# A transformer kernel with the filler matrix products at the heads of its attention stages removed

## The chip, the cores and the metric

The kernel runs on one core of one Trainium2 chip. The metric is device time in microseconds (us): the kernel before took 1113.98 us, the median of three runs (1110.98 to 1114.39). A core has five engines with queues of their own that meet only at semaphores: TensorE (PE in the profile, its weight loads PEld), VectorE (DVE), ScalarE (ACT), GpSimd (POOL) and SyncE (SP), which here only starts DMAs. TensorE's clock is granted at one of two levels, 1.2 or 2.4 GHz; the profile writes them 0.5 and 1.0.

## The reference

The input x is 2 x 1024 x 256 in float32; a context of 77 tokens per batch is attended to. Four layers follow each other, each with a cross attention and a feed-forward part:

```python
x = x + tanh(g_xattn[0]) * L0_xattn(layernorm(x), ctx)          # one head, no projections
x = x + tanh(g_ffn[0])   * L0_ffn(layernorm(x))                 # FP4 quantised gate, up, down
x = x + tanh(g_xattn[1]) * L1_xattn(layernorm(x), ctx, ctx)     # 16 heads of 16
x = x + tanh(g_ffn[1])   * L1_ffn(layernorm(x))                 # 256 -> 1024 -> 256, relu
x = x + tanh(g_xattn[2]) * L2_xattn(layernorm(x), ctx)          # 16 heads of 64
x = x + tanh(g_ffn[2])   * L2_ffn(layernorm(x))                 # one matrix, plus low rank
x = x + tanh(g_xattn[3]) * L3_xattn(layernorm(x), ctx, ctx)     # 16 heads of 16
x = x + tanh(g_ffn[3])   * L3_ffn(layernorm(x))                 # 16 experts and a shared one
```

An attention computes, per head, softmax(q k / sqrt(width)) v, and then an output projection.

## The kernel before

x stays in SBUF for the whole run, as 16 tiles of 128 rows. The program is a sequence of stages, and each engine runs through them in the same order: the start (layer 0's attention and the preparation of weights), `ffn0`, attention 1 (`att_tensor` and its fellows with l = 1), `ffn1`, attention 2 together with layer 2's feed-forward part (`att2_tensor` and its fellows), attention 3 (`att_tensor` with l = 3), and the mixture of experts. At the end of a stage each engine drains, raises a semaphore and waits until all five have done so (`end_stage`, L234 to L239; the profile shows these waits as L236).

Inside an attention stage each engine runs `pipeline` (L94): `step(t, p)` for t = -1, 0, 1, ... where `has(t)` tells whether a tile of that number exists. Steps up to 3 and the last ones are written out, the ones between run in a loop. The order of work on an engine is the program order, and there is no planner.

In `att_tensor`, step -1 turns the first normalised tile (two transposes, L373) and makes its queries (`queries`, L1216, eight products). ScalarE takes the queries' high part (`qT_hi`, L1304), VectorE the low part (`xT_lo`, L1351), and only then can the scores of tile 0 start. Step 0 turns tile 1, computes the scores of tile 0 in three pieces (`scores`, L1203, twelve products) and makes the queries of tile 1 (L1216). VectorE takes the maxima and subtracts them (L1362, L1363), ScalarE takes exponentials (L1319), and the low part of tile 1's queries stands in VectorE's order behind these. Step 1 begins with `wait_ge(tr_copied)` on exactly that low part. From step 1 on a step also turns the probabilities of the tile before (L373), multiplies them with the values (L1245), and from step 2 on projects (L1227, L1228).

In `att2_tensor`, step -1 turns the first tile (L1501); ScalarE makes `xT_hi` (L1545), VectorE `xT_lo` (L1608). Step 0 computes the scores of tile 0 (L1441, eighteen products) and turns tile 1 (L1501). Step 1 waits for tile 1's `xT_lo`. Later steps also turn the probabilities (L1451) and multiply them with the folded values (L1463).

At the end of a step with t < 1, and in `att2_tensor` also ahead of the pipeline, TensorE runs `keep_busy(pe, n)` (L884 to L887): n products of the bfloat16 tiles `ones3` (96 x 128) and two rows of `brow` (96 x 512) into bank 7 of PSUM. They wait for nothing, raise no semaphore, and nothing reads what they write: the next real product into bank 7 starts with `start=True`. There are 38 of them: 3 and 8 in attention 1 (steps -1 and 0), 4, 4 and 8 in attention 2 (ahead of the pipeline and in steps -1 and 0), 3 and 8 in attention 3.

Of the kernel before, what the change touches and what calls it, by code (L numbers as in the profile page):

```python
# [16 lines left out]
D = 256  # L17
# [65 lines left out]
def has(t):  # L83

    return not isinstance(t, int) or 0 <= t < T

def wait(eng, sem, value):

    if not (isinstance(value, int) and value <= 0):  # L90
        eng.wait_ge(sem, value)
# [21 lines left out]
def flamingo(nc, x_in, ctx_t, ctx_r, gates, tables, attn_in, bias_rows, fp4_in, ffn1_in, ffn2_in, moe_in,  # L113
             v_pairs, out):
    with ExitStack() as stack:
        enter = stack.enter_context

        def sb(name, shape, dt=F32):
            return enter(nc.sbuf_tensor(name, shape, dt))
# [7 lines left out]
        ones3 = sb("ones3", [96, P], BF16)  # L127
# [8 lines left out]
        brow = sb("brow", [96, NB * D], BF16)  # L136
# [83 lines left out]
        bank = [psum[:, 512 * n:512 * n + 512] for n in range(8)]  # L220
# [660 lines left out]

            return range((t - 1) * NPARTS // T, t * NPARTS // T) if 1 <= t <= T else range(0)

        def keep_busy(pe, n):  # L884

            for _ in range(n):
                pe.matmul(bank[7][:, 0:2 * D], ones3[:], brow[:, 0:2 * D], start=True, stop=True)  # L887

        def start_tensor(pe):
            s, tr, un = a_s[0], Count(), Count(set_s["filled"])  # L890

# [298 lines left out]
        def att_tensor(pe, l):  # L1190
            s, tr = a_s[l], Count()
            no, nt, vw = len(OUT_BANKS[l]), H * WIDTH[l] // P, VW[l]
            row = {1: 0, 3: 4}[l]

            def scores(t, p, j):
                h0, h1 = SCORE_BANKS[j]
                wait(pe, s["s_read"], 3 * t - 2 + j)
                col = (t // TB) * HK + h0 * SK
                parts = [(k, max(h0, 8 * k), min(h1, 8 * k + 8)) for k in range(KD)
                         if max(h0, 8 * k) < min(h1, 8 * k + 8)]  # L1200
                for k, a, z in parts:
                    for i, (q_, key) in enumerate(three((qT_hi[p], xT_lo[p]), (kb_hi[l], kb_lo[l]))):
                        last = pe.matmul(bank[j][:, (a - h0) * SK:(z - h0) * SK], q_[:, k, :],  # L1203
                                         key[:, bass.ds(col + (a - h0) * SK, (z - a) * SK)],
                                         start=(k, a, z) == parts[0] and i == 0,
                                         stop=(k, a, z) == parts[-1] and i == 2, skip_group_check=True)
                last.then_inc(s["s_ready"], 1)

            def queries(p, unit):

                pe.wait_ge(s["tr_copied"], unit)
                wait(pe, s["tr_copied"], tr.n - 1)
                dst = bank[TR34[tr.odd]]
                for j in range(KD):
                    for k in range(KD):
                        last = pe.matmul(dst[:, j * P:(j + 1) * P], Wq[l][:, k, j * P:(j + 1) * P], xnT[p][:, k, :],  # L1216
                                         start=j == 0 and k == 0, stop=j == KD - 1 and k == KD - 1,
                                         skip_group_check=True)
                last.then_inc(s["tr_filled"], 1)
                tr.up()  # L1220

            def project(t, unit):

                pe.wait_ge(s["tr_copied"], unit)
                wait(pe, s["y_read"], t - 2)
                for k in range(nt):
                    pe.matmul(bank[7][:, 0:D], onormT[:, k, :], Wo[l][:, k, :], start=k == 0, stop=False)  # L1227
                pe.matmul(bank[7][:, 0:D], ones3[:], brow[:, row * D:(row + 1) * D], start=False,  # L1228
                          stop=True).then_inc(s["y_ready"], 1)

            def values(t, p, units):

                v0 = ((t - 1) // TB) * KT * 3 * vw
                chunks = 0
                for g, k, a, z in value_items(l):
                    mine = [w[1] for w in value_items(l) if w[0] == g]
                    h0, a0 = OUT_BANKS[l][g][0], tile_heads(k)[0]
                    if k == mine[0]:

                        wait(pe, s["on_ready"], no * (t - 1) + g - 1)  # L1240
                    if k // 4 == chunks:
                        pe.wait_ge(s["tr_copied"], units[chunks])
                        chunks += 1
                    dst = bank[5 + (g + 1 - p) % 2][:, (a - h0) * vw:(z + 1 - h0) * vw]
                    last = pe.matmul(dst, probT[:, k, :],  # L1245
                                     Vb[l][:, bass.ds(v0 + (k * 3 + a - a0) * vw, (z - a + 1) * vw)],
                                     start=k == mine[0], stop=k == mine[-1], skip_group_check=True)
                    if k == mine[-1]:
                        last.then_inc(s["o_ready"], 1)

            def step(t, p):
                if has(t):
                    pe.wait_ge(s["tr_copied"], tr.n)
                if has(t + 1):
                    pe.wait_ge(s["xn_ready"], t + 2)
                    transposes(pe, s, tr, [(xn[1 - p][:, k * P:(k + 1) * P], P) for k in range(KD)], TR34)
                    xn_unit = tr.n
                if has(t):
                    scores(t, p, 0)
                    scores(t, p, 1)  # L1260
                if has(t - 2):
                    pe.wait_ge(s["on_ready"], t - 1)
                    transposes(pe, s, tr, [(onorm[:, k * P:(k + 1) * P], P) for k in range(nt)], TR34)
                    on_unit = tr.n
                units = []
                for j in range(3):
                    if has(t) and j == 1:
                        scores(t, p, 2)
                    if has(t - 1):
                        if j == 0 and isinstance(t, int) and t == 1:  # L1270
                            pe.wait_ge(pads_zero, {1: 4, 3: 6}[l])
                        if j == 0:
                            pe.wait_ge(s["exp_done"], t)
                        transposes(pe, s, tr, [(prob[1 - p][:, k * P:(k + 1) * P], P) for k in range(*PT_CHUNKS[j])],
                                   TR34)
                        units.append(tr.n)
                if has(t - 2):
                    project(t, on_unit)
                if isinstance(t, int) and t == T - 1:
                    front_turn(pe, l, 0)  # L1280
                if has(t + 1):
                    queries(1 - p, xn_unit)
                if has(t - 1):
                    values(t, p, units)
                if isinstance(t, int) and t == T - 1:
                    front_turn(pe, l, 1)
                if isinstance(t, int) and t == T:
                    for j in range(2, GT):
                        front_turn(pe, l, j)
                if isinstance(t, int) and t < 1:  # L1290
                    keep_busy(pe, 3 if t < 0 else 8)

            pipeline(pe, -1, step, [(tr, 2 * UNITS)], T + 1, AHEAD)
            if l == 3:
                router_logits(pe, 0)
            end_stage(pe, "pe")
# [134 lines left out]
        def att2_tensor(pe):  # L1431
# [52 lines left out]
            def step(t, p):  # L1484
                for j in range(3):
                    if has(t):
                        if j == 0:
                            pe.wait_ge(s["x_lo"], t + 1)
                        scores(t, p, j)
                    if j == 0 and has(t - 3):  # L1490
                        turn_second(t - 3)
                    if has(t - 1):
                        if j == 2 and isinstance(t, int) and t == 1:
                            pe.wait_ge(pads_zero, 6)
                        turn_probabilities(t - 1, 1 - p, j)
                if has(t - 3):
                    second(t - 3)
                if has(t + 1):
                    pe.wait_ge(s["xn_ready"], t + 2)
                    for k in range(KD):  # L1500
                        last = pe.transpose(x2_bank[:, k * P:(k + 1) * P], xn[1 - p][:, k * P:(k + 1) * P],  # L1501
                                            ident[:])
                    last.then_inc(s["x_filled"], 1)
                if has(t - 1):
                    outputs(t - 1, 1 - p)
                if isinstance(t, int) and t < 1:
                    keep_busy(pe, 4 if t < 0 else 8)

            keep_busy(pe, 4)
            pipeline(pe, -1, step, [(Count(), 0)], T + 2, AHEAD)  # L1510
            end_stage(pe, "pe")

# [1009 lines left out]
```

## Time and profile before

| | |
|---|---|
| median of three runs | 1113.98 us |
| profiled execution, its time | 1115.46 us |
| profiled execution, its span (first to last instruction) | 1113.7 us |
| mean granted clock of TensorE in it | 0.986 |
| TensorE busy | 1049.1 us (94%), 6222 products |
| VectorE busy | 786.0 us (71%) |
| ScalarE busy | 517.6 us (46%) |
| heads of the attention stages, first filler product | 270.7, 500.5, 677.1 us |

The page cuts the span into 40 slices of 27.8 us and gives each engine's busy share in tenths. The timeline and the windows used below have times in us from the start of the span. A busy time of TensorE counts overlapping products once. In the timeline, products of one form that stand next to each other are merged, so a row has a start, the length of the whole, and the count; "[0.71 <-DVE xT_lo L1351]" at the end says that the engine was idle for 0.71 us before it and what released it.

### The profile page before, as it was taken

Reading aid. Unit: us, or ns where it says so; the run is one execution under the profiler, and the core shown is the slowest. Engines: PE = TensorE matmul, PEld = TensorE weight load, DVE = VectorE, ACT = ScalarE, POOL = GpSimd, SP = SyncE. Lnnn points to the kernel's source line nnn. Section 1 sums busy time; section 2 is a strip of 40 time slices with the busy share of each in tenths; the row PEclk is TensorE's granted clock in tenths of the full one; section 3 lists DMA queues with packets and bytes.
Section 4 is the critical chain, followed back from the end, with each engine's and each line's share of the span. In section 5 each row is a group of like instructions: output and inputs, shape, how many; then the busy total and the mean of one; then the engine's idle time right before and its main releaser. Section 6 shows DMA issues by size and latency. Waiting matters only on the chain.

```text
span 1113.7 us, 18644 instructions
## 1 busy us (share of the span) xinstructions
PE 1049.1 (94%) x6222; PEld 899.6 (81%) x6222; DVE 786.0 (71%) x1809; ACT 517.6 (46%) x1196; POOL 164.1 (15%) x227
## 2 busy tenths in 40 slices
PE   4887899998999999999999997999989999999998
PEld 3755567776999978887888886999868888888887
DVE  5787879987787845458888867888655575565544
ACT  3676544433555555545544543565542433333322
POOL 2232000000112142230111001123331010000000
PEclk9899899999999989999999999999999999999999
DMA  9401010002000000000000005000022121222120
GB/s 277 113 1 41 1 12 1 1 1 77 1 1 0 2 12 1 1 1 1 1 0 0 1 1 241 1 0 1 1 73 66 54 78 56 58 75 64 51 86 29
DMA packets 30376, 41.22 MB, mean 37 GB/s; under 512 B 13615, under 2 KB 19577, under 8 KB 29414
## 3 DMA queue, kind: packets, MB, share of 16 engines
q1 hardware_dynamic: 29437, 39.63, 11.4%
q10 hardware_dynamic: 873, 0.72, 0.3%
q8 instruction: 39, 0.64, 0.2%
q14 instruction: 27, 0.22, 0.1%
HBM read 37.80 MB, written 2.54 MB: 36 GB/s over the span
## 4 chain that ended last, share of the span: by engine, by line
PE 51%; DVE 2%; ACT 1%; DMA 0%; issue 0%; PEldq 0%; POOL 0%; DVEq 0%; POOLq 0%; SPq 0%; PEld 0%; ACTq 0%
PE psum L2082 17%; PE psum L2093 8%; PE psum L1463 6%; PE psum L1441 5%; PE psum L1245 3%; PE psum L1203 3%; PE psum L373 2%; PE psum L1451 2%; PE psum L1227 1%; PE psum L1216 1%; PE psum L1480 1%; PE psum L2037 0%; PE psum L1501 0%; DMA work<-expert_shares 0%; PE psum L1472 0%
## 5 line engine op out<-in xcount | busy, mean ns | idle before, releaser
L298 POOL TENSOR_TENSOR rstd<-ve,mhalf 128x1 f32<-128x1 f32 x128 | 83.5, 653 | 697.2 <-DVE ve L293 697.2
L384 ACT COPY work<-psum 128x256 f32<-128x256 f32 (+2 forms) x241 | 99.5, 438 | 134.9 <-PE psum L373 130.0
L373 PE MATMUL psum<-ident,work 128*128 128x128 f32 (+2 forms) x596 | 97.2, 287 | 14.6 <-DVE xT_lo L1351 4.3
L2225 DVE TENSOR_TENSOR work<-psum,work 128x512 f32<-128x512 f32 x68 | 46.9, 690 | 74.8 <-ACT work L2156 74.7
L2164 ACT CAST h_hi<-work 128x512 fp32r<-128x512 f32 x68 | 42.2, 621 | 122.1 <-DVE work L2235 95.4
L373 PEld LDWEIGHTS psum<-ident,work 128*128 128x128 f32 (+2 forms) x596 | 74.5, 149 | 28.8 <-DVE xT_lo L1351 6.2
L2082 PE MATMUL psum<-x_hi,ew_hi 128*128 128x512 f32 (+1 forms) x272 | 87.2, 402 | 0.2
L2082 PE MATMUL psum<-x_lo,ew_hi 128*128 128x512 f32 (+1 forms) x272 | 85.3, 395 | 0.0
L2082 PE MATMUL psum<-x_hi,ew_lo 128*128 128x512 f32 (+1 forms) x272 | 84.9, 393 | 0.0
L1662 PE MATMUL psum<-early,work 128*128 128x352 f32 x256 | 81.4, 473 | 3.3 <-ACT zone L597 2.8
L2093 PE MATMUL psum<-ew_hi,h_hi 128*128 128x256 f32 x272 | 76.4, 281 | 2.3 <-DVE h_lo L2242 2.3
L2093 PE MATMUL psum<-ew_hi,h_lo 128*128 128x256 f32 x272 | 76.7, 282 | 0.0
L2093 PE MATMUL psum<-ew_lo,h_hi 128*128 128x256 f32 x272 | 76.3, 281 | 0.0
L2242 DVE TENSOR_TENSOR h_lo<-work,h_hi 128x512 fp32r<-128x512 f32 x68 | 47.0, 690 | 41.6 <-ACT h_hi L2164 41.5
L1245 PEld LDWEIGHTS psum<-zone,work 128*128 128x128 f32 x640 | 74.0, 192 | 0.2
L1245 PE MATMUL psum<-zone,work 128*128 (+2 forms) x640 | 74.2, 273 | 0.0
L1662 PEld LDWEIGHTS psum<-early,work 128*128 128x128 f32 x256 | 49.0, 197 | 29.2 <-ACT zone L597 3.6
L2156 ACT ACTIVATE work<-psum 128x512 f32<-128x512 f32 x68 | 40.6, 597 | 68.8 <-PE psum L2082 68.5
L1463 PE MATMUL psum<-zone,work 128*128 128x256 f32 (+1 forms) x320 | 71.7, 379 | 0.0
L1463 PEld LDWEIGHTS psum<-zone,work 128*128 128x128 f32 x320 | 59.6, 190 | 7.6
L1531 ACT ACTIVATE work<-psum,small 128x77 f32<-128x77 f32 x256 | 62.5, 380 | 3.9 <-DVE small L1565 3.9
L1362 DVE TENSOR_REDUCE small<-psum 128x6 f32<-128x462 f32 (+1 forms) x96 | 55.6, 580 | 9.0 <-PE psum L1203 9.0
(275 smaller groups left out, 2543.2 us busy)
## 6 DMA issues: line engine op xcount, KB each, us to landing
work<-expert_shares SPq DMA_DIRECT2D x64, 256.0 KB, 3.2
early<-in_experts_in SPq DMA_DIRECT2D x1, 6528.0 KB, 18.0
x<-in_x_in SPq DMA_DIRECT2D x4, 512.0 KB, 7.8
early<-in_W_in SPq DMA_DIRECT2D x2, 1024.0 KB, 6.0
out_x<-x SPq DMA_DIRECT2D x3, 512.0 KB, 4.3
early<-in_Wk SPq DMA_DIRECT2D x1, 1024.0 KB, 7.2
early<-in_Wq SPq DMA_DIRECT2D x1, 1024.0 KB, 9.0
zone<-in_Wv SPq DMA_DIRECT2D x1, 1024.0 KB, 13.8
```

What stands on the lines that cost most here:

```text
L298: pool.tensor_tensor(rstd[:, slot:slot + 1], ve[:, slot:slot + 1], mhalf[:, 0:1], ALU.pow).then_inc(s["rstd_ready"], 1)
L373: last = pe.transpose(dst[0:rows, at:at + n], src, ident[0:n, 0:n])
L384: act.copy(dst, src).then_inc(s["tr_copied"], 1)
L1245: last = pe.matmul(dst, probT[:, k, :], Vb[l][:, bass.ds(v0 + (k * 3 + a - a0) * vw, (z - a + 1) * vw)], start=k == mine[0], stop=k == min ...
L1362: link(dve, dve.tensor_reduce(mx[:, h0:h1], sc, AX_X, ALU.max))
L1441: last = pe.matmul(bank[j][:, 0:n], x_[:, k, :], a[k][0][:, bass.ds(col + a[k][1], n)], start=i == 0 and k == 0, stop=i == 2 and k == KD - 1)
L1463: pe.matmul(bank[6][:, 0:D], probT2[p][:, k, :], vo[:, bass.ds(v0 + k * D, D)], start=k == 0, stop=False, skip_group_check=True)
L1531: last = act.activation(prob[p][:, h * SK:(h + 1) * SK], bank[j][:, (h - h0) * SK:(h - h0 + 1) * SK], ACT.Exp, bias=nmx[:, h:h + 1])
L1662: last = pe.matmul(bank[c][:, 0:HALF], xnT[1 - p][:, k, :], wguT[:, k, c * HALF:(c + 1) * HALF], start=k == 0, stop=k == 1)
L2082: last = pe.matmul(bank[2 * which + e % 2][:], weights(w, e, which, k), a[:, k, cols], start=n == 0, stop=n == len(passes) - 1)
L2093: last = pe.matmul(bank[6 + j // 2][:, (j % 2) * D:(j % 2 + 1) * D], h[slot(e)][:, j * P:(j + 1) * P], weights(w, e, 2), start=e == 0 and ...
L2242: dve.tensor_tensor(h_lo[slot(e)][:], hf[e % 2], h_hi[slot(e)][:].bitcast(F32), ALU.subtract).then_inc(s["h_ready"], 1)
```

## The change

The calls of `keep_busy` in both functions and its definition are taken out. Nothing else changes.

```diff
-        def keep_busy(pe, n):
-
-            for _ in range(n):
-                pe.matmul(bank[7][:, 0:2 * D], ones3[:], brow[:, 0:2 * D], start=True, stop=True)
@@ step of att_tensor, at its end
-                if isinstance(t, int) and t < 1:
-                    keep_busy(pe, 3 if t < 0 else 8)
@@ step of att2_tensor, at its end, and ahead of its pipeline
-                if isinstance(t, int) and t < 1:
-                    keep_busy(pe, 4 if t < 0 else 8)
-
-            keep_busy(pe, 4)
             pipeline(pe, -1, step, [(Count(), 0)], T + 2, AHEAD)
```

## Rows read from the trace of the kernel before

**Rows 1.** The page: busy time of each engine, and the slices of TensorE's clock.
```profile
PE 1049.1 (94%) x6222; PEld 899.6 (81%) x6222; DVE 786.0 (71%) x1809; ACT 517.6 (46%) x1196; POOL 164.1 (15%) x227
PEclk9899899999999989999999999999999999999999
```
**Rows 2.** Windows: stretch, length, busy us per engine, TensorE's clock (PEclk), DMA share, GB/s.
```profile
285.00:380.00 95.00, 95.00 (x753) 90.90 (x753) 76.71 (x190) 49.75 (x102) 14.49 (x22) 1.00 0.00 1
```
**Rows 3.** Instructions of L887: duration in ns, minimum, median, maximum.
```profile
L887 PE MATMUL psum<-brow,ones x38: 376/379/390, 270.7 to 683.1; 96*128 96x512 bf16 x38
```
**Rows 4.** Timeline at the head of attention 1, TensorE.
```profile
268.79 0.44 PE L373 MATMUL psum<-ident,work 128*128 128x128 f32 x2 [0.63 <-DVEq L236]
...
269.75 1.16 PE L1216 MATMUL psum<-work,zone 128*128 128x128 f32 x8 [0.52 <-ACT work L384]
...
272.26 0.44 PE L373 MATMUL psum<-ident,work 128*128 128x128 f32 x2 [0.71 <-DVE xT_lo L1351]
...
274.36 1.05 PE L1216 MATMUL psum<-work,zone 128*128 128x128 f32 x8
...
278.55 0.44 PE L373 MATMUL psum<-ident,work 128*128 128x128 f32 x2 [1.41 <-DVE xT_lo L1351]
```
**Rows 5.** Timeline at the head of attention 2, TensorE and one row of VectorE.
```profile
500.52 1.04 PE L887 MATMUL psum<-brow,ones 96*128 96x512 bf16 x4 [2.06 <-SPq L236]
...
500.88 0.41 DVE L313 TENSOR_SCALAR work<-x,rstd,small 128x256 f32<-128x256 f32 x1
...
501.39 0.38 PE L1501 MATMUL psum<-ident,work 128*128 128x128 f32 x2
...
502.75 0.70 PE L1441 MATMUL psum<-a_hi,xT_hi 128*128 128x462 f32 x2
...
506.23 0.38 PE L1501 MATMUL psum<-ident,work 128*128 128x128 f32 x2
506.45 1.89 PE L887 MATMUL psum<-brow,ones 96*128 96x512 bf16 x8
...
509.59 0.68 PE L1441 MATMUL psum<-a_hi,xT_hi 128*128 128x462 f32 x2 [1.25 <-DVE xT_lo L1608]
```
**Rows 6.** Timeline at the head of attention 3, TensorE.
```profile
680.67 1.05 PE L1216 MATMUL psum<-work,zone 128*128 128x128 f32 x8
...
684.88 0.44 PE L373 MATMUL psum<-ident,work 128*128 128x128 f32 x2 [1.43 <-DVE xT_lo L1351]
```
**Rows 7.** Windows of stretches in which TensorE waited; columns as in rows 2.
```profile
82.90:86.30 3.40, 0.90 (x6) 0.56 (x4) 3.23 (x9) 0.86 (x5) 2.55 (x7) 1.00 0.00 0
...
127.30:130.70 3.40, 1.39 (x7) 0.77 (x5) 3.30 (x6) 3.24 (x10) 0.00 (x0) 1.00 0.00 0
803.20:806.60 3.40, 1.75 (x8) 1.08 (x9) 1.37 (x4) 2.41 (x5) 0.00 (x0) 1.00 0.00 0
86.40:89.80 3.40, 3.40 (x12) 3.09 (x13) 2.37 (x6) 2.58 (x9) 0.00 (x0) 0.50 0.00 0
820.30:823.70 3.40, 1.68 (x8) 1.02 (x6) 1.49 (x5) 0.77 (x2) 0.04 (x1) 1.00 0.79 278
499.40:502.80 3.40, 2.17 (x11) 1.00 (x11) 2.74 (x9) 0.37 (x1) 0.76 (x3) 1.00 0.03 7
```
**Rows 8.** Timeline of TensorE at the head of ffn1: the clock rises at 403.8.
```profile
401.02 1.06 PE L1881 MATMUL psum<-xg_lo,w_hi 128*128 128x512 f32 x2
401.88 1.06 PE L1881 MATMUL psum<-xg_hi,w_lo 128*128 128x512 f32 x2
...
404.64 0.63 PE L1881 MATMUL psum<-xg_hi,w_hi 128*128 128x512 f32 x2
405.10 0.63 PE L1881 MATMUL psum<-xg_lo,w_hi 128*128 128x512 f32 x2
```
**Rows 9.** Windows, columns as in rows 2: the longest stretch at the low clock after the start.
```profile
45.50:52.20 6.70, 6.70 (x30) 6.59 (x30) 1.43 (x6) 2.58 (x7) 0.28 (x1) 0.50 0.00 0
```
**Rows 10.** The window's products against the identity (transposes): length, TensorE, its weight loads, clock, DMA.
```profile
55.70:59.10 3.40, 2.12 (x15) 1.37 (x14) 1.00 0.00 0
```

## The prediction

> **What bounds the kernel now.** I read the page first: TensorE is busy for 94% of the span, and its clock is at the full level in nearly every slice [rows 1]. The windows over the running part of attention 1 say the same: TensorE is busy for 95.00 of 95 us, VectorE for 76.71 [rows 2]; attentions 2 and 3 look alike. So once a stage is under way, whatever TensorE loses there arrives at the end. The heads of the stages are different. There the timeline shows TensorE waiting for VectorE, and the removed products stand in these waits, so I looked at three things: how long each wait would be without them, what the granted clock did elsewhere after such waits, and what a stretch at the low clock costs.
>
> **The removed work by itself.** 38 products of 379 ns [rows 3]; next to each other they start about 0.22 us apart (eight in 1.89 us, 1.89 - 0.38 = 1.51 over seven steps [rows 3, 5]). That is 38 x 0.22 = 8.4 us of array time. None of it is on the path, with one exception:
> - Attention 1, step -1: after the three fillers TensorE still waits 0.71 us for `xT_lo`; step 0: after the eight it still waits 1.41 us [rows 4].
> - Attention 3, step 0: still 1.43 us [rows 6], and its step -1 repeats attention 1's.
> - Attention 2: 1.25 us is left after the eight [rows 5], and the four of step -1 end some 0.3 us before the scores start at 502.75.
> - The exception is the four ahead of the pipeline: they start at 500.52 and the transposes behind them at 501.39, 0.87 us later. But the tile that these turn is written from 500.88 to 501.29 [rows 5], so the transposes can start only 0.1 us earlier.
>
> Cost of the work itself: a gain of 0.1 us, between 0 and 0.87. Nothing waits on the fillers, no semaphore or DMA moves, and the wait that ends each stretch stays the same `xT_lo`. If this were all, nothing measurable would happen.
>
> **What takes the fillers' place: idle time.** Ends and starts from rows 4 to 6:
> - Attention 1, step 0: the queries end at 274.36 + 1.05 = 275.41, the next product starts at 278.55: 3.14 us.
> - Attention 3, step 0: 681.72 to 684.88: 3.16 us.
> - Attention 2, step 0: 506.61 to 509.59: 2.98 us.
> - Attention 2, head: TensorE has been idle since 500.52 - 2.06 = 498.46; from there to 502.75, in 4.29 us, only two transposes of 0.38 us are left.
> - Step -1 of attentions 1 and 3: from 268.79 - 0.63 = 268.16 to 272.26, 4.1 us with 0.44 + 1.16 = 1.60 us of work, in attention 3 the same.
>
> **What the clock does after such waits.** At the full level, stretches of 3.4 us in which TensorE was busy for 0.90, 1.39 and 1.75 us were each followed by a fall to 1.2 GHz, one of 1.68 us was not, and the head of attention 2, with its fillers at 2.17 us, was not [rows 7]. None of the waits of before at the full clock is as long as the three bare ones above: with them, a stretch of that length holds under 0.5 us of work if it lies on the wait, less than in any of rows 7. So I expect a fall at each step 0 and at the head of attention 2, and about an even chance in each step -1, whose 1.60 us lies between the row that fell at 1.75 and the one that held at 1.68.
>
> The Trainium skill ("TensorE: Matmul & The Clock Gate", section on why this matters) advises against idle gaps of more than about 3 us; two of the bare waits are just over, one is just under. Read strictly it would leave these falls in doubt; that is the first rival. The trace is harsher than the page: the wait in 82.90 to 86.30 was 2.5 us, and the clock fell. The same page (part 4) says that transposes don't count as the engine's work in the way products do. Read so, step -1 would hold only the queries' 1.16 us and fall more surely. The trace doesn't bear that out: in 55.70 to 59.10 TensorE's work was 2.12 us of transposes and hardly anything else, and the clock stayed at 1.00 [rows 10]. I leave the chance even.
>
> **What a fall costs.** The shortest stretch at the low clock is 3.4 us, as 86.40 to 89.80, where TensorE is then busy throughout [rows 7]. The same pair of 512-column products starts every 0.86 us at the low clock (401.02, 401.88) and every 0.46 us at the full one (404.64, 405.10) [rows 8]. A fully used stretch of 3.4 us thus does 3.4 x 0.46 / 0.86 = 1.8 us of full-clock work: it loses 1.6 us. If part of it lies in the wait, that part costs nothing; if the engine finds too little to do, the low clock goes on for 6.7 us [rows 9] and costs up to 3.1 us.
> - Each step 0: the fall comes inside the wait or shortly after its end; then step 1 keeps TensorE busy without a stop. Between 0 and 3.1 us; I take 1.2, three quarters of the 1.6, as about a quarter of the stretch should lie in the wait. Three times: 3.6 us.
> - Head of attention 2: the scores of tile 0, 502.75 to 506.23 at the full clock, run at half. Behind them stand the maxima, the exponentials and `xT_lo` of tile 1, which ends the next wait, so nearly the whole delay goes on. Between 0 and 3.1 us; I take 1.3.
> - Step -1 of attentions 1 and 3: the scores of tile 0 slow down, but VectorE's chain behind them is as long as they are. 0.6 us each when it falls, half the time: 0.6 together (0 to 3.1).
> - The fillers themselves: -0.1.
>
> Sum: 3.6 + 1.3 + 0.6 - 0.1 = 5.4 us. Against the profiled execution's own time of 1115.46 that is 1120.9. The median of the timed runs lies 1.5 us lower, so I forecast **1119.4 us**. By the lower bounds the sum is -0.9, by the upper ones 3 x 3.1 + 3.1 + 3.1 = 15.5.
>
> **Rivals.**
> - *The clock holds* (for it: 820.30 to 823.70 held with 1.68 us of work [rows 7]; against it: the bare waits hold far less). Then only -0.1 is left: 1113.9 us.
> - *Falls, but mostly hidden*: they come early in the waits, or at steps where VectorE is the slower one anyway (71% busy overall [rows 1]). Two falls of 1.2 us remain: 1116.3 us.
> - *The low clock stays on*: the heads have more waits, so a fallen clock finds too little work to rise again, as in 45.50 to 52.20 [rows 9]. Four places at 3.1 us: 12.4 us, 1126.4 us. Step 1 with its unbroken work speaks against it.
> - *Faster*: by earlier or later starts the falls that before has at stage ends (as after 803.20 to 806.60 [rows 7]) vanish, at 1.6 us each; there are four such in the trace, at the ends of attentions 1 and 3 and the stages behind them. This decides only if all bare waits also stay without a fall and at least three of these go: 1109.1 us. Those falls stem from waits that the change doesn't touch.
> - *Nothing happens because the fillers did nothing*: the same as the first rival, and counted there.
>
> **How the numbers follow.** A difference under 0.3% (3.3 us, so 1110.6 to 1117.3) can't be told from none. Chances: forecast 0.64 (own range 1117.3 to 1124), clock holds 0.13, mostly hidden 0.12, stays low 0.07, faster 0.04. Slower: 0.64 + 0.07 = 0.71; within: 0.25; faster: 0.04. The range 1113.0 to 1124.0 takes in the forecast, the hidden case and most of the first rival; outside are the low clock that stays, the faster case, and the edges.
>
> **What would show it.** Right: the windows over 277 to 284, 500 to 514 and 683 to 690 of the new trace have PEclk 0.50 for 3.4 us or more each; the timeline has idle times of about 3.1, 3.0 and 3.2 us before the first product of step 1; the first step of each stage is 1 to 2 us longer, and the later steps are unchanged. Wrong: the idle times are there and the clock stays at 1.00 in two or more of the four places, or it falls and the step's end is not later, which would make VectorE the path at the heads.

## The result and the profile after

| | before | after |
|---|---|---|
| median | 1113.75 us (6 runs, 1110.83 to 1114.39) | 1119.20 us (6 runs, 1118.36 to 1120.28) |
| profiled execution | 1115.46 us | 1119.74 us |
| span | 1113.7 us | 1117.9 us |
| mean granted clock | 0.986 | 0.979 |

The ratio after to before is 1.0061, with a 95% interval of 1.0047 to 1.0075. The medians differ by 5.4 us. The ratio, by which noise is judged, stands for 6.8 us (5.2 to 8.4): slower, clear of noise, by well under 2%.

The page after, its first part and the clock; they answer to [rows 1]. TensorE has 38 products less, and two more slices, the 10th and the 25th, have a lower clock digit.

```profile
PE 1048.3 (94%) x6184; PEld 901.6 (81%) x6184; DVE 785.7 (70%) x1809; ACT 517.4 (46%) x1196; POOL 164.1 (15%) x227
PEclk9899899998999989999999998999999999999999
```

Timeline of TensorE at the heads of the three stages after (start, length, what, count, idle time before it and what ended it). The rows answer to [rows 4], [rows 5] and [rows 6]; ten lines were taken out, so `scores` of attention 1 is L1198 now, `queries` L1211, and attention 2's transposes and scores are L1494 and L1434.

```profile
268.79 0.44 PE L373 MATMUL psum<-ident,work 128*128 128x128 f32 x2 [0.63 <-DVEq L236]
269.74 1.16 PE L1211 MATMUL psum<-work,zone 128*128 128x128 f32 x8 [0.52 <-ACT work L384]
272.26 0.69 PE L373 MATMUL psum<-ident,work 128*128 128x128 f32 x2 [1.36 <-DVE xT_lo L1344]
...
276.08 1.91 PE L1211 MATMUL psum<-work,zone 128*128 128x128 f32 x8
279.51 0.45 PE L373 MATMUL psum<-ident,work 128*128 128x128 f32 x2 [1.51 <-DVE xT_lo L1344]
...
286.68 0.41 PE L373 MATMUL psum<-ident,work 128*128 128x128 f32 x2
...
501.34 0.44 PE L1494 MATMUL psum<-ident,work 128*128 128x128 f32 x2 [2.06 <-SPq L236]
503.36 1.12 PE L1434 MATMUL psum<-a_hi,xT_hi 128*128 128x462 f32 x2 [1.58 <-DVE xT_lo L1598]
...
508.39 0.38 PE L1494 MATMUL psum<-ident,work 128*128 128x128 f32 x2
511.44 0.68 PE L1434 MATMUL psum<-a_hi,xT_hi 128*128 128x462 f32 x2 [2.67 <-DVE xT_lo L1598]
...
676.96 0.44 PE L373 MATMUL psum<-ident,work 128*128 128x128 f32 x2 [0.69 <-POOLq L236]
...
680.44 0.44 PE L373 MATMUL psum<-ident,work 128*128 128x128 f32 x2 [1.36 <-DVE xT_lo L1344]
...
687.32 0.44 PE L373 MATMUL psum<-ident,work 128*128 128x128 f32 x2 [2.17 <-DVE xT_lo L1344]
...
695.92 0.42 PE L373 MATMUL psum<-ident,work 128*128 128x128 f32 x2
```

The queries of tile 1 took 1.05 us [rows 4] and take 1.91 now, and the first pair of attention 2's scores took 0.70 [rows 5] and takes 1.12. That is the low clock. The windows of the same profile show its stretches (stretch, length, busy time of the engines, then TensorE's clock):

```profile
271.30:278.10 6.80, 5.73 (x22) 5.28 (x22) 4.37 (x10) 0.71 (x4) 0.00 (x0) 0.50 0.59 248
503.40:506.80 3.40, 3.40 (x9) 2.97 (x10) 0.74 (x2) 0.07 (x1) 0.20 (x1) 0.50 0.00 0
680.90:684.30 3.40, 3.40 (x14) 3.26 (x14) 2.19 (x4) 0.37 (x1) 0.00 (x0) 0.50 0.74 323
687.70:691.10 3.40, 3.40 (x15) 3.19 (x14) 2.06 (x4) 0.37 (x1) 0.00 (x0) 0.50 1.12 481
```

Where the time of this execution went can be read stage by stage, from a stage's first product to the first product of a later step:

| from, to | before | after | longer by |
|---|---|---|---|
| attention 1: first transposes to step 1 | 268.79 to 278.55 | 268.79 to 279.51 | 0.96 |
| the same to step 2 | to 285.56 | to 286.68 | 1.12 |
| attention 2: first product to step 1 | 500.52 to 509.59 | 501.34 to 511.44 | 1.03 |
| attention 3: first transposes to step 1 | 675.12 to 684.88 | 676.96 to 687.32 | 0.60 |
| the same to step 2 | to 691.89 | to 695.92 | 2.19 |

1.12 + 1.03 + 2.19 = 4.3 us, and the spans differ by 4.2 us. The rest of the kernel gave and took a few tenths. The rows of the timeline of before that the table and the experiments need, and that are not among [rows 4] to [rows 6] (first products of step 2 of attention 1, of attention 3, and of step 2 of attention 3; 514.16 is the turn of tile 2 in step 1 of attention 2):

```profile
285.56 0.42 PE L373 MATMUL psum<-ident,work 128*128 128x128 f32 x2
...
514.16 0.38 PE L1501 MATMUL psum<-ident,work 128*128 128x128 f32 x2
...
675.12 0.44 PE L373 MATMUL psum<-ident,work 128*128 128x128 f32 x2 [0.69 <-POOLq L236]
...
691.89 0.42 PE L373 MATMUL psum<-ident,work 128*128 128x128 f32 x2
```

### The profile page after: what moved, and what is told of

It is laid out like the page before. It is cut to its first block, busy times and chain, and to the rows that moved or that the text cites. A ratio compares the mean times of both kernels' runs of the same rounds, so it can differ in the third digit from the quotient of the medians.

```text
span 1117.9 us, 18569 instructions
## 1 busy us (share of the span) xinstructions
PE 1048.3 (94%) x6184; PEld 901.6 (81%) x6184; DVE 785.7 (70%) x1809; ACT 517.4 (46%) x1196; POOL 164.1 (15%) x227
## 4 chain that ended last, share of the span: by engine, by line
PE 86%; DVE 6%; ACT 4%; issue 1%; SPq 1%; DMA 1%; POOL 0%; PEldq 0%; DVEq 0%; POOLq 0%; ACTq 0%; PEld 0%
PE psum L2072 17%; PE psum L2083 8%; PE psum L1652 7%; PE psum L373 6%; PE psum L1456 6%; PE psum L1240 6%; PE psum L1198 5%; PE psum L1434 5%; PE psum L1871 4%; PE psum L1887 4%; PE psum L1660 4%; PE psum L1222 3%; PE psum L1211 2%; PE psum L1444 2%; PE psum L1473 1%
## 5 line engine op out<-in xcount | busy, mean ns | idle before, releaser
L1355 DVE TENSOR_REDUCE small<-psum 128x6 f32<-128x462 f32 (+1 forms) x96 | 55.6, 580 | 10.9 <-PE psum L1198 10.7
```

The source lines that it names most:

```text
L1355: link(dve, dve.tensor_reduce(mx[:, h0:h1], sc, AX_X, ALU.max))
```

## The experiments

All were timed in alternation with the kernel before. Ratios are to before, with 95% intervals.

| kernel | fillers left | median us | ratio | mean clock of its runs |
|---|---|---|---|---|
| before (three groups of runs) | 38 | 1112.66, 1112.40, 1111.68 | | 0.985 to 0.987 |
| e13, the whole change again | 0 | 1118.87 | 1.0060 (1.0041 to 1.0079) | 0.977 |
| e1, attention 2 bare | 22 | 1111.67 | 1.0002 (0.9986 to 1.0018) | 0.984 |
| e2, attentions 1 and 3 bare | 16 | 1116.71 | 1.0036 (1.0022 to 1.0049) | 0.979 |
| e3, 16 columns wide | 38 narrow | 1117.06 | 1.0046 (1.0029 to 1.0064) | 0.979 |
| e4, transposes instead | 76 transposes | 1111.74 | 1.0003 (0.9989 to 1.0017) | 0.986 |
| e5, step 0 bare | 14 | 1117.69 | 1.0053 (1.0032 to 1.0074) | 0.979 |
| e6, step -1 bare | 24 | 1113.50 | 1.0010 (0.9994 to 1.0027) | 0.982 |
| e10, only step 0 of 1 and 3 | 16 | 1113.89 | 1.0012 (0.9996 to 1.0027) | 0.982 |
| e11, four in each step 0 | 26 | 1119.68 | 1.0061 (1.0039 to 1.0083) | 0.979 |
| e7, more at stage ends | 38 + 17 | 1111.34 | 0.9997 (0.9982 to 1.0011) | 0.985 |
| e9, as e7, attention 2 bare | 22 + 17 | 1110.91 | 0.9989 (0.9976 to 1.0002) | 0.987 |
| e12, as e7, 8 in the experts | 38 + 25 | 1111.15 | 0.9996 (0.9984 to 1.0007) | 0.987 |

Over all 201 runs of this table a straight line through time against mean clock falls by 5.7 us for each 0.01 of clock, with a correlation of -0.79. That line runs through different kernels; among the runs of one kernel, taken together, it falls by 3.9 us at a correlation of -0.58. 0.01 of the clock is half speed for 2% of 1112 us, 22 us. By the first line about a quarter of a low stretch's length is lost, where a fully used stretch would lose nearly half. That many stretches lie where TensorE waits or is not the bound, the start above all, would explain it, but was not measured.

### e3: the same instructions, hardly any work in them

```diff
-                pe.matmul(bank[7][:, 0:2 * D], ones3[:], brow[:, 0:2 * D], start=True, stop=True)
+                pe.matmul(bank[7][:, 0:16], ones3[:], brow[:, 0:16], start=True, stop=True)
```

> All 38 fillers stay where they are, with their weight loads, but each is 16 columns wide instead of 512. Clock theory: the array has almost nothing to do in the waits, so the falls come as if the fillers were gone: 1117.5 to 1120.5 us, with low stretches at the heads of the three stages. Rival (what counts is that instructions are issued and weights loaded in the waits, or where they stand): as before, 1113.7 us.

Measured: 1.0046. The interval excludes 1 and takes in the whole loss of 1.0061; at its lower end it is half of that. This separates the two theories: 38 instructions with their weight loads in the same places, each of 16 columns, hold a quarter of the gain by the ratio and half at most. The timeline of its attention 3 shows the narrow products, and the step after at the low clock:

```profile
681.91 0.35 PE L887 MATMUL psum<-brow,ones 96*128 96x16 bf16 x8
684.32 0.49 PE L373 MATMUL psum<-ident,work 128*128 128x128 f32 x2 [2.06 <-DVE xT_lo L1351]
...
692.92 0.42 PE L373 MATMUL psum<-ident,work 128*128 128x128 f32 x2
```

```profile
684.60:688.00 3.40, 3.40 (x16) 3.21 (x14) 1.86 (x3) 0.37 (x1) 0.00 (x0) 0.50 1.13 492
```

From step 1 to step 2 it takes 692.92 - 684.32 = 8.60 us where before takes 691.89 - 684.88 = 7.01: 1.6 us for this fall.

### e4: transposes as fillers

```diff
-                pe.matmul(bank[7][:, 0:2 * D], ones3[:], brow[:, 0:2 * D], start=True, stop=True)
+                for k in range(2):
+                    pe.transpose(bank[7][:, k * P:(k + 1) * P], ident[:], ident[:])
```

Measured: 1.0003, no loss. The timeline of the head of attention 1 and its windows:

```profile
268.60 0.82 PE L888 MATMUL psum<-ident 128*128 128x128 f32 x6
...
273.09 1.91 PE L888 MATMUL psum<-ident 128*128 128x128 f32 x16
276.41 0.44 PE L373 MATMUL psum<-ident,work 128*128 128x128 f32 x2 [1.40 <-DVE xT_lo L1352]
```

```profile
266.60:270.00 3.40, 2.25 (x16) 1.78 (x16) 1.62 (x6) 1.00 (x3) 1.19 (x4) 1.00 0.70 207
...
273.40:276.80 3.40, 2.00 (x18) 1.76 (x17) 2.74 (x9) 3.03 (x4) 0.89 (x2) 1.00 0.02 5
```

Sixteen transposes take the 1.9 us of eight fillers, and the clock stays at 1.00. The Trainium skill ("TensorE: Matmul & The Clock Gate", part 4) says that the full clock doesn't engage for the transpose mode, since it doesn't count as TensorE being busy in the same way. Here the trace disagrees, and the measurement decides: transposes kept a clock that was at the full level as products do. Whether transposes alone would raise a low one, no run here tried. This profile has one fall at the head of attention 2 (497.4 to 500.9), in spite of the transposes there. Fillers of products weren't a complete protection either: see e7 and e11.

### e1 and e2: attention 2, or attentions 1 and 3

```diff
@@ e1, in att2_tensor
-                if isinstance(t, int) and t < 1:
-                    keep_busy(pe, 4 if t < 0 else 8)
-            keep_busy(pe, 4)
@@ e2, in att_tensor
-                if isinstance(t, int) and t < 1:
-                    keep_busy(pe, 3 if t < 0 else 8)
```

> The 16 fillers of attention 2 are gone, the 22 of attentions 1 and 3 stay. Clock theory (what the fillers do is keep the granted clock up, and the whole loss is the work done at the low clock after a fall): the profile has a fall within 498 to 512 us and none from 268 to 285 or from 676 to 690; attention 2's first product of step 1 comes 1 to 1.6 us later, counted from the start of the stage, and the time is 1 to 2.5 us above before, a quarter to a half of the whole change's 5.4. Rival (the fillers hold the instruction stream in a favourable place, whatever the clock does): the loss follows the number of fillers, 16 of 38, so 2.3 us, and it needs no fall.

> The 22 fillers of attentions 1 and 3 are gone, the 16 of attention 2 stay. Clock theory: falls at the heads of attentions 1 and 3 and none in attention 2; together with the kernel without attention 2's fillers the two losses add up to the whole change's 5.4 us within a microsecond; here 3 to 4.5 us. Rival (place in the instruction stream): 22 of 38, so 3.1 us, also where no fall stands in the profile.

Measured: e1 1.0002, below what I expected, e2 1.0036, as expected. The two add up to 0.38%, against 0.61% of the whole; their intervals just allow that. The windows of e1 show both what the clock does and why attention 2 loses little:

```profile
496.80:500.20 3.40, 3.40 (x9) 2.97 (x10) 0.69 (x2) 0.02 (x1) 0.23 (x1) 0.50 0.00 0
501.40:504.80 3.40, 0.78 (x6) 0.54 (x5) 3.15 (x10) 2.81 (x12) 0.25 (x1) 1.00 0.02 5
```

There is one fall at the head, on the scores of tile 0, and none behind the wait of step 0, though TensorE worked for only 0.78 of 3.4 us there. The same holds for the profiles of after, e3, e9 and e10: with the head bare, the head falls, and step 0's wait is passed without a fall. In e13 both fell. The fall at the head costs 1.0 us (as in the table above); that is within e1's interval, which reaches to 2.0 us. Why its median shows nothing of it is not settled. The profiles differ in falls elsewhere too: before has four at the ends of attentions 1 and 3 and in the stages behind them (from 390.2, 400.4, 796.4 and 806.6), e1 one (800.6).

e2 has the longest low stretch outside the start of the kernel, 13.6 us from the end of attention 2 to the end of attention 3's step 0. It began 2.9 us ahead of the stage whose fillers were gone (attention 3 starts at 674.38), so it is not their absence that started it:

```profile
671.50:685.10 13.60, 10.74 (x37) 8.64 (x37) 7.33 (x21) 1.68 (x6) 1.74 (x3) 0.50 0.76 305
```

### e5 and e6: step 0, or step -1

```diff
@@ e5, in both functions: the calls for t == 0 go
-                if isinstance(t, int) and t < 1:
+                if isinstance(t, int) and t < 0:
@@ e6, in both functions: the calls for t == -1 go, and keep_busy(pe, 4) ahead of attention 2's pipeline
-                if isinstance(t, int) and t < 1:
+                if isinstance(t, int) and t == 0:
```

> Only the fillers of step 0 (8 in each stage) are removed; those of step -1 and the four ahead of attention 2's pipeline stay. If the bare waits of 3 us in step 0 are what matters, as my prediction had it (3.6 of its 5.4 us), the time is 2.5 to 4 us above before. If the gaps of step -1 matter more, as the profile of the changed kernel suggests (there both stages fell already in step -1, and attention 1 then had no fall of its own after step 0), it is under 1.5 us above.

> Only the fillers of step -1 (3 in attentions 1 and 3, 4 in attention 2) and the four ahead of attention 2's pipeline are removed; the eight of step 0 stay. By my prediction 0.6 for the two step -1 gaps and 1.3 for attention 2's head: 1 to 2.5 us above before. If step -1 is the main place: 2.5 to 4 us above. If the two parts share their falls (a clock that fell in step -1 can't fall again in step 0), this and the kernel without step 0's fillers sum to more than the 5.4 us of the whole change.

Measured: e5 1.0053, nearly the whole loss; e6 1.0010. Step 0 is the place that counts, and the correction that I had drawn from the profile after was wrong. The timeline of e5, first products of steps 1 and 2 of attention 1, of step 1 of attention 2 and its turn of tile 2, and of steps 1 and 2 of attention 3:

```profile
276.04 0.69 PE L373 MATMUL psum<-ident,work 128*128 128x128 f32 x2 [3.15 <-DVE xT_lo L1351]
...
285.65 0.42 PE L373 MATMUL psum<-ident,work 128*128 128x128 f32 x2
...
506.87 0.69 PE L1441 MATMUL psum<-a_hi,xT_hi 128*128 128x462 f32 x2 [2.98 <-DVE xT_lo L1608]
...
513.01 0.38 PE L1501 MATMUL psum<-ident,work 128*128 128x128 f32 x2
...
683.73 0.44 PE L373 MATMUL psum<-ident,work 128*128 128x128 f32 x2 [3.16 <-DVE xT_lo L1351]
...
692.35 0.41 PE L373 MATMUL psum<-ident,work 128*128 128x128 f32 x2
```

```profile
275.30:282.10 6.80, 6.07 (x24) 5.54 (x24) 4.65 (x11) 2.04 (x4) 0.98 (x2) 0.50 0.00 0
507.40:510.80 3.40, 3.40 (x12) 2.92 (x11) 2.95 (x8) 1.02 (x5) 0.00 (x0) 0.50 0.00 0
684.90:688.30 3.40, 3.40 (x17) 3.33 (x17) 3.30 (x7) 0.59 (x1) 0.00 (x0) 0.50 1.13 492
```

The bare waits are 3.15, 2.98 and 3.16 us, as worked out from before, and there is a fall at each of the three. The step behind them takes 9.61 us in attention 1 (285.65 - 276.04) where before takes 7.01: 2.6 us, with a low stretch of 6.8 us. In attention 3 it takes 8.62: 1.6 us. In attention 2 the turn of tile 2 comes 6.14 us behind the start of the step (513.01 - 506.87), where before takes 4.57 (514.16 - 509.59): 1.6 us again. The three make 5.8 us, near the 5.3 us between the medians. The profiled execution itself was the fastest of the six, 1113.50 us: it has none of the four falls at stage ends that before's has.

e6 fell at the head of all three stages as well (windows of its profile):

```profile
269.10:275.90 6.80, 5.84 (x23) 5.46 (x24) 4.37 (x10) 0.71 (x3) 0.00 (x0) 0.50 0.60 251
...
501.20:504.60 3.40, 3.40 (x9) 2.97 (x10) 0.75 (x2) 0.07 (x1) 0.21 (x1) 0.50 0.02 5
```

But these stretches lie on the scores of tile 0 and the wait behind them, where VectorE's chain takes about as long, so they cost no more than 1.1, 1.0 and 0.6 us: the stages reach step 2 (attention 2: step 1) that much later after their first product than in before. Together that is 2.8 us where the runs show 1.1 (-0.7 to 3.0 by the interval); e10's profile has the same three falls, for 2.6 us.

### e10 and e11: how many are needed

```diff
@@ e10, in att_tensor; att2_tensor's are all removed
-                if isinstance(t, int) and t < 1:
-                    keep_busy(pe, 3 if t < 0 else 8)
+                if isinstance(t, int) and t == 0:
+                    keep_busy(pe, 8)
@@ e11, in both functions (att2_tensor has 4 for t < 0)
-                    keep_busy(pe, 3 if t < 0 else 8)
+                    keep_busy(pe, 3 if t < 0 else 4)
```

> Of the 38 fillers only the 16 in step 0 of attentions 1 and 3 are left. If the loss sits in these two places, as the kernels measured so far say (without step 0's fillers 1.0053 of before, without step -1's 1.0010, without attention 2's 1.0002): 0 to 2 us above before. If each group had its own price, 22 of 38 fillers gone would cost about 3 us.

> Four fillers instead of eight in each step 0, the others as before. Where the clock is what counts, the array's work in the wait matters and not that there is something: four fillers (0.9 us of 3 us) leave a wait that is partly bare, so some of the falls come back: 1 to 3.5 us above before. If any activity in the wait were enough, the time is that of before; if only an unbroken array keeps the clock, it is that of all of step 0's fillers removed, 5 us above.

Measured: e10 1.0012, so sixteen of the 38 hold all but a fifth of the gain (by the interval, at least half). e11 1.0061, worse than I expected: with four fillers in each wait of 3 us the loss is that of having none, within the interval. Its profile explains this only in part. Attention 1 passed the wait of step 0 without a fall, attention 2 did not, and in attention 3 the clock was low from 678.0, at the start of the stage and with step -1's three fillers in place, and no fall came behind step 0. That is one of three waits, and the loss of four fillers stands on the six timed runs and their mean clock of 0.979. The timeline and windows of its attention 2, and below them the same for attention 3:

```profile
507.67 1.03 PE L887 MATMUL psum<-brow,ones 96*128 96x512 bf16 x4
510.81 1.14 PE L1441 MATMUL psum<-a_hi,xT_hi 128*128 128x462 f32 x2 [2.12 <-DVE xT_lo L1608]
```

```profile
507.40:510.70 3.30, 1.30 (x8) 0.55 (x6) 2.84 (x10) 2.76 (x13) 0.19 (x1) 1.00 0.02 5
510.80:514.20 3.40, 3.39 (x10) 2.96 (x11) 3.04 (x8) 0.03 (x1) 0.26 (x1) 0.50 0.00 0
```

```profile
689.50 0.44 PE L373 MATMUL psum<-ident,work 128*128 128x128 f32 x2 [1.94 <-DVE xT_lo L1351]
```

```profile
678.00:684.80 6.80, 6.20 (x22) 4.41 (x23) 2.16 (x7) 1.37 (x4) 0.55 (x1) 0.50 0.97 371
```

### e13: the whole change again

> The changed kernel again, so that it is timed on the same chip as the next three and gives one more profile. 5 to 6.5 us above before. The profiles so far say that falls are shared: where a fall comes in step -1, the low stretch of 6.8 us ends in the bare wait of step 0 and no second fall follows there (attention 1), so at most two low stretches per stage. A theory by which each bare wait costs on its own would want 3 + 3 falls in attentions 1 to 3.

Measured: 1.0060. Its profile has another pattern than the first: attention 1 falls in step -1 and again after step 0, attention 2 falls at the head and again after step 0, and in attention 3 one stretch runs from 677.5 to 687.8. So "at most two low stretches per stage" held, but my theory that a fall in step -1 rules out one after step 0 did not. As a tendency it stands. Counted over all 14 profiles:

| what stands in step 0's wait | waits | followed by a fall |
|---|---|---|
| eight products, or sixteen transposes | 22 | 0 |
| nothing, the head's fillers in place (e5) | 3 | 3 |
| nothing or narrow products, the head at the low clock before (after, e13, e1, e2, e3, e9, e10) | 14 | 4 |
| four products (e11) | 3 | 1 |

```profile
278.20:285.00 6.80, 6.15 (x24) 5.54 (x24) 4.66 (x11) 2.54 (x4) 0.98 (x2) 0.50 0.00 0
...
510.30:513.70 3.40, 3.01 (x10) 2.59 (x10) 3.04 (x9) 0.16 (x1) 0.55 (x1) 0.50 0.00 0
677.60:687.70 10.10, 8.22 (x32) 7.34 (x32) 5.07 (x13) 1.37 (x4) 0.55 (x1) 0.50 1.01 408
```

### e7, e9 and e12: fillers where before still falls

```diff
@@ att_tensor, step; keep_busy has the bank as a third argument
+                if isinstance(t, int) and t == T:
+                    keep_busy(pe, 3, 6)
                 if has(t - 2):
                     ...
+                if isinstance(t, int) and t == T + 1:
+                    keep_busy(pe, 2, 6)
@@ behind its pipeline
+            keep_busy(pe, 4 if l == 1 else 3, 6)
@@ e12 only: the experts' group, first one, ahead of its first down products
+                    if first and e == 2:
+                        keep_busy(pe, 8)
```

> The kernel before with 9 (attention 1) and 8 (attention 3) further fillers at the stage ends: three at the start of the step after the last scores, two behind the last turned tile and four or three behind the last projection, where the trace of before shows waits of 0.56, 0.46 and 0.96 us and falls behind them. Clock theory: the falls at 386 to 404 and 793 to 810 us become rarer; each costs up to 1.6 us and there were four in the profile of before: 1 to 3 us below before. Rival: the fillers lie partly on the path (the three at the step's start are 0.65 us in a wait of 0.56), the products there are bound by other things, and the time is within 1 us of before or above.

> The fillers at the stage ends as in the kernel before this one in the list, and attention 2's 16 fillers removed, which by themselves measured 1.0002 of before. If the parts are independent: the same as with the stage ends alone, within 1 us. If attention 2's fillers cover falls that other places had hidden so far, it is 1 to 2 us slower than that kernel.

> All fillers of before, those at the ends of attentions 1 and 3 (0.9997 of before by themselves), and eight more in the mixture of experts in front of its first down product, where TensorE waits for 2.25 us and the profiles of three kernels have a fall. Clock theory: that fall, 1.6 us where it comes, goes: 1 to 3 us below before. Rival: the wait there ends before the eight (1.73 us) are through in some runs, or the fall is rare: no difference.

Measured: 0.9997, 0.9989 and 0.9996; none is clear of 1, and the 1 to 3 us that I had expected of e7 and e12 were not seen (the intervals reach to 2.0 and 1.8 us). None of the three profiles has a low stretch at the end of attentions 1 or 3, but neither have those of e5 and e10, without such fillers. So the falls there come in a part of the executions only, and taking them out moves the median by less than these runs can tell. No version was shown to beat the kernel before.

The profiles of e7 and e12 show another thing: the clock fell ahead of attention 3 and stayed low through the start of the stage, for 6.8 us in e7 and 10.2 in e12, although all the fillers of before stand there. The row is e7's three fillers of step -1, which take 1.48 us where the three in attention 1 of before take 0.81:

```profile
674.31 1.48 PE L887 MATMUL psum<-brow,ones 96*128 96x512 bf16 x3
```

```profile
668.90:675.60 6.70, 5.55 (x18) 3.21 (x16) 2.83 (x11) 1.00 (x3) 1.71 (x3) 0.50 0.69 249
```

## Why the prediction was right

The forecast was 1119.4 us, measured were 1119.2. The mechanism (idle time, a fall of the clock, slower steps behind it) was right, and several of its terms were not.

- *The removed work costs nothing on the path*: right. The wait that ends step 0 is the same `xT_lo` in every profile. The exception was misread. The transposes at the head of attention 2 turn tile 0, which had been written before the stage began; the VectorE row that I took for it [rows 5] writes tile 1. They started with the stage, at 501.34, so they gained the whole 0.87 us, and the scores behind them 0.2 us (503.36 - 501.34 = 2.02 against 502.75 - 500.52 = 2.23). The term was -0.1 and should have been -0.2.
- *The clock falls where the fillers were*: right, by e3 against e4: the same places filled with work keep it, with products of 16 columns most or all of the loss comes.
- *A fall at each step 0, 1.2 us each, 3.6 together*: the place was right where the head still had its fillers (e5, three of three). Not every execution of the whole change falls at all three: the profile after did once in three, e13 twice. The size was too small: 1.6 us in attentions 2 and 3, 2.6 in attention 1 (e5). I had taken a quarter off for the part that lies in the wait; in e5 the falls came 0.7 us before the end of the wait or after it, so the low stretch lay on step 1.
- *The head of attention 2, 1.3 us*: a fall in each profile in which its fillers were gone, for 1.2 us between the scores and step 1 and 1.0 net of the gain.
- *An even chance in each step -1, 0.6 us when it falls*: the chance rested on 1.60 us lying between the row that fell at 1.75 and the one that held at 1.68, but 1.60 lies below both. Without these fillers, or with narrow ones, the clock was low in step -1, or fell within 0.5 us behind it, in all 12 cases (attentions 1 and 3 of after, e13, e2, e3, e6 and e10); with them in 3 of 16 (attention 3 of e7, e11 and e12). By the first product of step 1 the falls had cost 1.0 and 0.6 us in after and 1.0 and 2.1 us in e13.
- *"If the engine finds too little to do, the low clock goes on for 6.7 us"*: [rows 9], cited for it, don't show it, as TensorE counts as busy there for 6.70 of 6.70 us. Stretches of that length did come behind the change: 6.8 us in attention 1 of after, with TensorE busy for 5.73.
- Falls at step 0 that I expected too often, at prices that were too low, and falls in step -1 that I expected too seldom came out together at 5.4 us forecast and 5.4 between the medians. That the point is so close is luck, also in the sample: by the ratio the loss is 6.8 us, and e13, the same kernel, gave 1118.87 against 1111.68, 7.2 us. The range was what the terms carried.

By my own test for "right", the prediction's picture of the places failed: two of its four, step 0 of attentions 1 and 2, had no fall behind them in the profile after, and the waits there were 1.51, 2.67 and 2.17 us and not 3.1, 3.0 and 3.2, since the work ahead of them ran at the low clock and grew into them. My test for "wrong" wasn't met either, as it asked for the long idle times. e5 alone shows the waits as forecast. A single profile is one draw of where the falls land; e13, the same kernel, drew another.

The rivals: that the clock holds fell with the result. That most falls are hidden is true of step -1, not of step 0. That the low clock stays on is partly true, for single stages (10.2 us in e13, 13.6 in e2). It cost less than the rival's 3.1 us a place: in e13 attention 3 reached step 1 2.1 us later than in before (11.90 us behind its first product, against 9.76). That falls at stage ends move was seen in single profiles and not in a median.

## What to carry to other kernels

Where TensorE is the bound and a stage's head makes it wait for other engines, look at the granted clock behind the wait before calling its idle time free: here three waits of 3 us cost 5 us in the steps after them (e5). Work without use in such a wait can hold the clock: in the waits of step 0, eight products of 512 columns or sixteen transposes did in all 22 cases, while with four products, or eight of 16 columns, the runs lost all or most of what they lose with none. Judge such a change by many timed runs, as one profile shows only one of the patterns in which the falls can land.

## What the hardware showed that I had not expected

- Float32 transposes keep the clock as products do (e4: 16 of them in 1.9 us, clock 1.00, ratio 1.0003).
- A weight load and a product of 16 columns, eight times in 0.35 us, do little or nothing for it (e3: 1.0046, 1.0029 to 1.0064).
- The effect of the fillers is not in proportion: with four of eight the loss is whole (1.0061, 1.0039 to 1.0083), with eight it is gone. Where it falls, one profile of e11 can't say.
- The same wait of the same kernel is followed by a fall in one execution and not in another (step 0 of attention 2: none in the profile after, one at 510.3 in e13).
- A low stretch that began in a stage with waits went on for 10.2 us (e13) and 13.6 us (e2), while TensorE was busy for 8.2 of 10.1 and 10.7 of 13.6 us. Stretches of 6.8 and 10.2 us came with all fillers in place (e7, e12).
